# Attention: values times probabilities with two small products for three, and the parts added on ScalarE and VectorE once per group

## The reference, cut to what matters

```
q = X @ Wq.T + bq;  k = encoder_output @ Wk.T + bk;  v = encoder_output @ Wv.T + bv
q = q.reshape(b, LQ, G, HPG, HD).transpose(0, 2, 3, 1, 4)      # G = 8 groups, HPG = 4 heads, HD = 16
scores = einsum('bgrqd,bgkd->bgrqk', q, k) / sqrt(HD)          # causal and padding masks: -inf
w = softmax(scores, axis=-1)
out = einsum('bgrqk,bgkd->bgrqd', w, v)                        # this product is what changes
x = x + tanh(g_xattn[0]) * (out @ Wo.T + bo)
```

## Time and profile before

| | us |
|---|---|
| median of 3 runs | 1865.72 |
| lowest and highest | 1864.51, 1871.24 |
| the profiled execution's own time | 1870.31 |
| its span (first to last instruction) | 1868.6 |
| mean granted clock of TensorE | 0.954 of full |

### The profile page before, as it was taken

The page is one execution under the profiler, slowest core; times in us unless marked ns, Lnnn a source line. Parts: engine busy times, 40 slices in busy tenths (PEclk is TensorE's granted clock), DMA queues, the critical chain, the costliest instruction groups (busy, mean ns, idle before and its releaser), DMA issues. The chain is left out here.

```text
span 1868.6 us, 29908 instructions
## 1 busy us (share of the span) xinstructions
PE 1629.5 (87%) x11050; PEld 845.9 (45%) x11050; DVE 975.4 (52%) x1975; ACT 711.5 (38%) x1311; POOL 824.9 (44%) x853
## 2 busy tenths in 40 slices
PE   4699998999847888976999987999999999788897
PEld 3255555565423343432656643444444444334343
DVE  5566676677435777762556552267554333111136
ACT  2187778778843545441223221121111111222221
POOL 2387787767733444442354334343342531111134
PEclk9799999999758999997999998999999999999999
DMA  5532322212414445333345425364453743466655
GB/s 183 128 87 70 86 70 78 69 45 53 93 28 82 102 99 102 80 77 65 69 110 108 101 55 134 87 145 107 101 122 86 157 107 69 101 153 153 156 148 169
DMA packets 423478, 188.36 MB, mean 101 GB/s; under 512 B 365020, under 2 KB 387806, under 8 KB 423336
## 3 DMA queue, kind: packets, MB, share of 16 engines
q1 hardware_dynamic: 417656, 167.84, 39.6%
q0 software_dynamic: 5680, 18.62, 4.0%
HBM read 77.17 MB, written 22.81 MB: 54 GB/s over the span
## 5 line engine op out<-in xcount | busy, mean ns | idle before, releaser
L993 POOL TENSOR_TENSOR a_pl<-a_prob,a_ph 128x512 f16<-128x512 f32 x256 | 295.5, 1165 | 113.6 <-ACT a_prob L902 112.4
L1076 DVE TENSOR_REDUCE a_mx<-bank 128x2 f32<-128x512 f32 x256 | 172.7, 686 | 101.0 <-PE bank L624 99.2
L137 PE MATMUL bank<-XTh,d_whs 128*128 128x512 f16 x512 | 195.3, 381 | 0.9 <-ACT e_y L2361 0.7
L138 PE MATMUL bank<-XTl,d_whs 128*128 128x512 f16 x512 | 195.3, 381 | 0.0
L139 PE MATMUL bank<-XTh,d_wls 128*128 128x512 f16 x512 | 195.1, 381 | 0.0
L901 ACT ACTIVATE a_ph<-bank 128x512 f16<-128x512 f32 x256 | 153.6, 600 | 88.4 <-PE bank L644 75.1
L2199 POOL CAST d_cut<-d_raw 128x512 f16<-128x512 f32 x90 | 58.0, 645 | 234.8 <-DMA d_raw<-in_L_ffn_sw 155.2
L902 ACT ACTIVATE a_prob<-bank 128x512 f32<-128x512 f32 x256 | 153.8, 601 | 0.0
L2119 DVE TENSOR_TENSOR d_hid<-d_hid,bank 128x512 f32<-128x512 f32 x64 | 44.0, 687 | 181.1 <-PE bank L139 171.4
L1332 PE MATMUL bank<-b_wfc,b_xTh 128*128 128x512 f16 x256 | 98.2, 384 | 32.8 <-DMA b_xTl<-f_cut 25.4
L1342 PE MATMUL bank<-b_wpj,b_hTh 128*128 128x512 f16 x256 | 104.6, 409 | 24.0 <-DMA b_hTl<-b_hcut 23.9
(11 more groups left out here) (330 smaller groups left out, 4040.3 us busy)
## 6 DMA issues: line engine op xcount, KB each, us to landing
d_raw<-in_L_ffn_w SPq DMA_DIRECT2D x48, 256.0 KB, 3.0
d_raw<-in_L_ffn_sw SPq DMA_DIRECT2D x42, 256.0 KB, 3.1
made<-e_y SPq DMA_DIRECT2D x39, 256.0 KB
a_stage<-in_L_ffn_w_fc SPq DMA_DIRECT2D x32, 256.0 KB, 2.8
a_stage<-in_L_ffn_w_proj SPq DMA_DIRECT2D x32, 256.0 KB, 3.0
a_fbuf<-in_ctx SPq DMA_DIRECT2D x16, 256.0 KB, 3.5
rows<-f_cut SPq DMA_DIRECT2D x16, 256.0 KB, 2.5
out_x<-X SPq DMA_DIRECT2D x16, 256.0 KB
```

Source lines behind the costliest of these rows:

```text
L137: nc.tensor.matmul(out_ap, lhi, rhi, start=first, stop=False)
L138: nc.tensor.matmul(out_ap, lhi, rlo, start=False, stop=False)
L993: nc.gpsimd.tensor_tensor(pl[:, n % NP, :], prob[:, n % 2, :], ph[:, n % NP, :], ALU.subtract).then_inc(ev["L"], 1)
L1076: nc.vector.tensor_reduce(mx[:, h, tt, half, 2 * (g % 4):2 * (g % 4) + 2], bank[BS + m % 2][:, :].rearrange("p (r k) -> p r k", r=2), AX_X ...
```

## The change

- `times_v`: two small products instead of three. `a_ph` is multiplied with all 33 columns at once, so that its product with the low values lands in 16 columns of its own, and `a_pl` with the first 17 as before. A head takes 33 columns of a bank where it took 17, so a bank holds one group, and the banks alternate with each group.
- ACT gets `low_values`, once per group: it copies the 16 low columns of 8 head-halves (128 elements per partition) from PSUM to `a_oa`, after the exponentials of step n with n % 4 == 3.
- DVE's `normalise` runs once per group, at n = 3, 7, 11, ... 31, ahead of the maxima of that step. It waits for `oc` from ACT's `low_values`, takes the reciprocal, adds the two parts (`a_ob`) and multiplies.

```diff
--- before.py
+++ after.py
@@ -360,14 +360,16 @@
     prob = sb("a_prob", [P, 2, D])
     ph = sb("a_ph", [P, NP, D], F16)
     pl = sb("a_pl", [P, NP, D], F16)
-    rec = sb("a_rec", [P, 2, 2, 8])
+    rec = sb("a_rec", [P, 2, 2, 4])
+    oa = sb("a_oa", [P, 2, 2, 4, HD0])
+    ob = sb("a_ob", [P, 2, 2, 4, HD0])
     on = sb("a_on", [P, 2, 2, D])
     oTh = sb("a_oTh", [P, 2, KC, P], F16)
     oTl = sb("a_oTl", [P, 2, KC, P], F16)
 
     names = ("Q0", "Q1", "KV0", "KV1", "hq0", "hq1", "lq0", "lq1", "hk0", "hk1",
              "lk0", "lk1", "hv0", "hv1", "lv0", "lv1", "tq", "tk", "cq", "ck", "S", "M", "nm",
-             "nt", "nc", "ng0", "ng1", "ST", "E", "L", "AV", "ON", "To0", "To1", "hO0", "hO1", "lO0", "lO1", "O0", "O1", "x0", "x1", "ch")
+             "nt", "nc", "ng0", "ng1", "ST", "E", "L", "AV", "ON", "oc", "To0", "To1", "hO0", "hO1", "lO0", "lO1", "O0", "O1", "x0", "x1", "ch")
     ev = {n: sem("a_" + n) for n in names}
     k_in, k_ch, k_pad, k_tr, k_m = (sem("k_" + n) for n in ("in", "chain", "pad", "tr", "mask"))
     k_bin, k_bhi, k_blo, k_bias = (sem("k_" + n) for n in ("bias_in", "bias_hi", "bias_lo", "bias"))
@@ -393,7 +395,7 @@
     TURN0, TURN1 = 19, 0
     NEG0, NEG1 = 18, 4
     OTURN, OUT = 5, (7, 8)
-    NORM = LAG + 8
+    NORM = LAG + 4
 
     NPIECE = 32
     ROUND = 12582912.0
@@ -648,26 +650,24 @@
             def times_v(b, n):
 
                 g, half, kc = n // 4, n // 2 % 2, n % 2
-                if n % 8 == 0:
-                    wait("ON", b, g // 2 + 1, G0 // 2)
+                if n % 4 == 0:
+                    wait("ON", b, g + 1, G0)
                 wait("L", b, n + 3, NS)
-                into = bank[BAV + g // 2 % 2]
+                into = bank[BAV + g % 2]
                 for r in range(2):
                     for qt in range(2):
-                        c = (((qt * 2 + g % 2) * 2 + r) * 2 + half) * (HD0 + 1)
+                        c = ((qt * 2 + r) * 2 + half) * VW
                         q = slice((2 * r + qt) * P, (2 * r + qt + 1) * P)
 
-                        first = n % 8 == 0 and r == 0 and qt == 0
-                        nc.tensor.matmul(into[:, c:c + HD0 + 1], ph[:, n % NP, q], vv[:, b % 3, kc, g, 0:HD0 + 1],
+                        first = n % 4 == 0 and r == 0 and qt == 0
+                        nc.tensor.matmul(into[:, c:c + VW], ph[:, n % NP, q], vv[:, b % 3, kc, g, :],
                                          start=first, stop=False, skip_group_check=True)
-                        nc.tensor.matmul(into[:, c:c + HD0], ph[:, n % NP, q], vv[:, b % 3, kc, g, HD0 + 1:VW],
-                                         start=False, stop=False, skip_group_check=True)
                         last = nc.tensor.matmul(into[:, c:c + HD0 + 1], pl[:, n % NP, q], vv[:, b % 3, kc, g, 0:HD0 + 1],
                                                 start=False, stop=(kc == 1), skip_group_check=True)
                 last.then_inc(ev["AV"], 1)
 
             def turn_output(b):
-                wait("ON", b, G0 // 2 + 2, G0 // 2)
+                wait("ON", b, G0 + 2, G0)
                 for tt in range(2):
                     for k in range(KC):
                         last = nc.tensor.transpose(bank[BM + tt][:, k * P:(k + 1) * P], on[:, b % 2, tt, k * P:(k + 1) * P],
@@ -836,6 +836,14 @@
                     act.wait_ge(ev[f"ng{h}"], 32 * b)
                 nc.scalar.activation(nT[:, h, :], bank16(BM)[0:H0 // 2, 0:2 * P], ACT.Copy).then_inc(ev["nc"], 1)
 
+            def low_values(b, g):
+                wait("AV", b, 4 * g + 4 + NP, NS)
+                if G0 * b + g >= 2:
+                    act.wait_ge(ev["ON"], G0 * b + g + 1)
+                nc.scalar.activation(oa[:, g % 2], bank[BAV + g % 2][:, 0:8 * VW]
+                                     .rearrange("p (t h c) -> p t h c", t=2, h=4)[:, :, :, HD0 + 1:VW], ACT.Copy)\
+                  .then_inc(ev["oc"], 1)
+
             def high_output(b):
                 for tt in range(2):
                     wait(f"To{tt}", b)
@@ -900,6 +908,9 @@
                     wait("L", b, n + 1, NS)
                     nc.scalar.activation(ph[:, n % NP, :], bank[BST + n % 2][:, :], ACT.Exp)
                     nc.scalar.activation(prob[:, n % 2, :], bank[BST + n % 2][:, :], ACT.Exp).then_inc(ev["E"], 1)
+                    if n % 4 == NORM % 4 and (b or n >= NORM):
+                        g = G0 * b + (n - NORM) // 4
+                        low_values(g // G0, g % G0)
                     if summed(b, n) is not None:
                         absolute(summed(b, n))
                     if cut_piece(b, n) is not None:
@@ -920,6 +931,7 @@
                         if n == PK[tt] + 1:
                             high_kv(b + 2, tt)
             bodies(body)
+            low_values(B - 1, G0 - 1)
             high_output(B - 1)
 
         @block.gpsimd
@@ -1008,7 +1020,7 @@
             def wait(n, b, count=1, per=1):
                 dve.wait_ge(ev[n], b * per + count)
 
-            PER = G0 // 2
+            PER = G0
             nlink = Chain(dve, n_ch)
             tlink = Chain(dve, t_ch)
 
@@ -1084,17 +1096,18 @@
                                             mx[:, h].rearrange("p t e j -> p (t e j)"), -1.0, None, ALU.mult)\
                       .then_inc(ev["nm"], 1)
 
-            def normalise(link, b, p):
-
-                wait("AV", b, 8 * p + 8 + NP, NS)
-                wait("ON", b, p + 1, G0 // 2)
-                o = bank[BAV + p % 2][:, 0:16 * (HD0 + 1)].rearrange("p (t h c) -> p t h c", t=2, h=8)
-                link(nc.vector.reciprocal(rec[:, p % 2], o[:, :, :, HD0]))
-                if b >= 2 and p == 0:
+            def normalise(link, b, g):
+
+                wait("oc", b, g + 1, G0)
+                wait("ON", b, g + 1, G0)
+                o = bank[BAV + g % 2][:, 0:8 * VW].rearrange("p (t h c) -> p t h c", t=2, h=4)
+                nc.vector.reciprocal(rec[:, g % 2], o[:, :, :, HD0])
+                link(nc.vector.tensor_tensor(ob[:, g % 2], o[:, :, :, 0:HD0], oa[:, g % 2], ALU.add))
+                if b >= 2 and g == 0:
                     wait("To1", b - 2)
-                nc.vector.tensor_tensor(on[:, b % 2, :, p * P:(p + 1) * P].rearrange("p t (h c) -> p t h c", h=8),
-                                        o[:, :, :, 0:HD0],
-                                        rec[:, p % 2].unsqueeze(3).broadcast_to([P, 2, 8, HD0]), ALU.mult)\
+                nc.vector.tensor_tensor(on[:, b % 2, :, 4 * HD0 * g:4 * HD0 * (g + 1)]
+                                        .rearrange("p t (h c) -> p t h c", h=4), ob[:, g % 2],
+                                        rec[:, g % 2].unsqueeze(3).broadcast_to([P, 2, 4, HD0]), ALU.mult)\
                   .then_inc(ev["ON"], 1)
 
             def low_output(b):
@@ -1173,9 +1186,9 @@
                     scales()
                 for n in range(NS):
                     if b and n == 3:
-                        normalise(old[0], b - 1, G0 // 2 - 1)
-                    if n >= NORM and (n - NORM) % 8 == 0:
-                        normalise(link, b, (n - NORM) // 8)
+                        normalise(old[0], b - 1, G0 - 1)
+                    if n >= NORM and (n - NORM) % 4 == 0:
+                        normalise(link, b, (n - NORM) // 4)
                     if b and n == OTURN + 1:
                         low_output(b - 1)
                     if b and n == OUT[1] + 1:
@@ -1205,7 +1218,7 @@
                     nc.vector.reduce_sum(sums[:, :], part[:, :].rearrange("p (m u) -> p m u", m=2), AX_X).then_inc(t_part, 1)
             old = [None]
             bodies(body)
-            normalise(old[0], B - 1, G0 // 2 - 1)
+            normalise(old[0], B - 1, G0 - 1)
             low_output(B - 1)
             residual(B - 1)
     st.close()
```

## The result

The changed kernel takes 1911.8 us (median of 4 runs, 1911.2 to 1913.9) where the kernel before took 1866.2 beside it (4 runs, 1864.5 to 1871.2): 1.0255 times as long, 95% interval 1.0236 to 1.0273. It is slower by 46 us. The prediction had 10 us slower, and a range that ended at 1885.

What follows compares the result with a forecast made beforehand. It took PE as mostly the bound in steps 0 to 24, ACT and POOL in 25 to 31. Bodies and end summed to +7.7 us, the clock +2.6, together +10.3 on 1865.7: 1876.0 us, range 1859 to 1885.

Steps and rivals of the forecast that it cites:

- DVE's new wait: Normalise waits for ACT's step-n exponentials and copy; at n = 31 maxima come 2.45 us later and L137 1.8 us later.
- Small products 26 ns apart with 33 columns: On PE, 33-column products follow each other at 25 ns, hardly depending on the clock, saving 0.10 us per step.
- The copy of 0.28 us: ACT makes 64 copies from PSUM, at most 0.28 us each, costing nothing in bodies 0 to 3, 1.2 us in body 7.
- the promised 25.6 us of PE: PE's saving of 0.10 us in each of 256 steps, counted only where PE is the bound.
- 0.68 us, between 0.62 and 0.95: On DVE, the new normalise of reciprocal, add and multiply would take 0.68 us, where the old one cost 0.62.
- Behind it on DVE stand the maxima of step n and all that follows.: DVE's new wait holds up the maxima of step n, for which PE's scores of step n+2 wait.
- This goes into the 1.3 us of L598: Maxima delayed 1.4 us at n = 11 and 15, holding PE some 0.6 us, are covered by PE's existing L598 wait.
- inside its lead of two steps: Waits at n = 23 and 27 hold PE 0.5 us each, covered because PE is up to two steps ahead.
- The clock, +2.6: Six new PE stalls of about 1.9 us in steps 6 and 7 bring two falls to half clock, 1.3 us each.
- The delay is absorbed: Rival: DVE's slack or PE's two banks cover the delay, L137 keeps its time; about -6, 1860 us; chance 0.15.
- 33 columns cost 56 ns: Rival: 33-column products on PE are dearer, so PE gains nothing; 1882 us; chance 0.08.
- The clock in every body: Rival: the clock falls in every body, from three falls on; +7.7 + 9.6, 1883 us; chance 0.15.

Runs made afterwards that it cites:

- run 5: run 4 with ACT's copy of the low columns moved ahead of the two exponentials of its step: 1858.2 us, 0.9972 of the kernel before.
- run 6: The changed kernel without copy and add, low-value product left out of the result, DVE waiting for PE only: 1854.6 us, 0.9954 of the kernel before.
- run 1: The changed kernel with the add's sum written back to PSUM and the multiply reading it there: 1899.2 us, 1.0197 of the kernel before.
- run 4: The changed kernel with the edits of Run 3 and run 1 together: 1864.4 us, 1.0012 of the kernel before.
- run 10: The changed kernel with DVE adding both parts by a reduction into SBUF, no ACT copy, waiting for PE only: 1870.0 us, 1.0041 of the kernel before.
- run 2: The changed kernel with `magnitude` moved ahead of the normalise: 1887.3 us, 1.0138 of the kernel before.
- run 11: run 7 with `magnitude` ahead of the normalise, part of the result left out: 1871.2 us, 1.0049 of the kernel before.
- Run 3: The changed kernel with the normalise behind `magnitude`, the maxima and the first take of its step: 1874.6 us, 1.0063 of the kernel before.
- run 7: run 6 plus DVE waiting, ahead of each normalise, for ACT's two exponentials of that step: 1888.6 us, 1.0125 of the kernel before.

## Why the prediction was wrong

The step that failed is the pricing of DVE's new wait. The prediction let it cost only at n = 31, through L137, and took for absorbed, or did not count, what stood behind it everywhere else: the maxima of the other steps, and `magnitude`, for which ACT waits. The runs show 13 to 17 us for the first and 17 to 20 us for the second. The normalise and the clock were mis-sized besides.

**Right.** Small products 26 ns apart with 33 columns, at either clock. The copy of 0.28 us (what it costs ACT was not measured by itself; it is within the 4 us between runs 5 and 6). The beginning of the mechanism: DVE waits for ACT in the same step, and the maxima are late. The sign of the whole, though in part by luck: it hung on L137, which in fact hardly waits. That the promised 25.6 us of PE would mostly not count: 8.7 by run 6, where ten steps per body were counted, so 7 or 8.

**"0.68 us, between 0.62 and 0.95" for a normalise.** It took 1.24 us from the reciprocal to the maxima at n = 31, 1.32 in step 3 of body 3 (267.29 to 268.61). The multiply was sized by a row with an operand in PSUM; the new one reads SBUF alone, and the nearest row for that, with one input and the output in SBUF, was L1083 at 1.12. This term was mis-sized, by about 0.5 us in each of 63 places, and it cost 8 to 10 us (runs 1, 4, 10), where the prediction added 3 us of work per body that "DVE has room for" and priced it only behind n = 31.

**"Behind it on DVE stand the maxima of step n and all that follows."** The prediction wrote this and then followed the maxima alone. In the steps with a piece of weights `magnitude` is in "all that follows" and ACT waits for it. The steps 11 and 23 of bodies 4 to 6 and nearly every normalise of body 7 stand in such steps. This closes a circle and was priced at nothing; it was worth 17 to 20 us (runs 2, 11), the largest part. Of the 33.6 us of bodies 4 to 7 the move of `magnitude` gives 18.3 back, and all of body 7's, which has no maxima. The earlier trace rows had the operation in it; it was used for the copy only.

**"This goes into the 1.3 us of L598", "inside its lead of two steps".** Late maxima at n = 11, 15, 23 and 27 were counted as covered, and only n = 31 as paid, at L137. In fact PE waits 40.7 us for maxima, in 43 places, and 1.3 at L137. Sorted by the step of the maxima that it waited for, 17.6 us belong to the steps from 23 to 28, which were to be "inside its lead of two steps", 7.6 us to those from 15 to 19, 12.1 us to 31, 3 and 4, and 3.4 us to those from 7 to 11. The wait at L598 (now L600), which was to take up the delays of 11 and 15, is 10.0 us in run 6 and 5.1 in the change, in six places: 0.8 us a body absorbed. Run 3 against 2 gives 13 us for the late maxima, run 11 against 6 gives 17; the forecast had 2.45 once per body less what was gained.

**The clock, +2.6.** Six more spells at half clock in bodies 0 to 6 instead of two, an estimate of 8 us for 2.6, and at most 16 with body 7. It is counted in the steps of the account and not beside them; that the further spells follow PE's further waits is argued, and no run holds the waits and changes the clock alone.

Of the rivals, none was it. "The delay is absorbed" is false by runs 3 and 7. "33 columns cost 56 ns" is false by the trace. The clock in every body is near in size, six further spells where it had six falls, but that rival gave 1883 and the time is 29 us above it.

## What to carry to other kernels

Where a change puts a wait into an in-order engine's list, write down every instruction behind it up to the next slack, and for each who waits for it, the engine waited for included: a wait of A for B in front of work that B needs makes a circle, and costs on both. Put the instruction that waits behind the work that others need; here this order alone took back 33 of 46 us. Size an operation by a row with the same operands in the same memories, not the same shape: beside a busy POOL, DVE's multiply from SBUF took up to 1.24 us and the one from PSUM 0.29.

## What the runs showed of the hardware that was not expected

- A small `tensor_tensor` of DVE with both operands in SBUF that started while POOL was at work waited for the end of POOL's operation each time, 63 of 63 (62 times a `tensor_tensor` of 1.16 us, once a cast of 0.61), and ended 0.15 us behind it; with one operand in PSUM (0.24 us) or the sum in PSUM (0.29 us, 64 of 64) never.
- A matmul with 33 columns, each with its weights loaded anew, follows the one before after 26 or 27 ns at full and at half clock alike.
- A reduction over pairs from PSUM into PSUM, 128x256 to 128x128, takes 0.38 us on DVE, and is a way to add two parts in one bank without another engine.
